# Sixteen-clip audio layer on one core: other steps let the table gathers go on GpSimd

## The reference

```python
q = (x @ Wq).reshape(b, n, HEADS, DIM) * DIM ** (-0.5)          # 8 heads of 64
sim = jnp.einsum('pbnhd,pkhd->pbnhk', qpk, pk_keys)             # two halves, 64 keys each
scores, idx = jax.lax.top_k(sim, 16)                            # 16 of 64 in each half
final_scores, pk_idx = jax.lax.top_k(all_sums, 16)              # 16 of the 256 pairs
final_scores = jax.nn.softmax(final_scores)
k = jnp.einsum('bnhk,bnhkd->bnhd', final_scores, keys_table[ind])
v = jnp.einsum('bnhk,bnhkd->bnhd', final_scores, values_table[ind])
out = causal_softmax(q, k) @ v, then @ Wo, plus the residual
```

## Time and profile before

| | |
|---|---|
| median of the three runs | 5366.33 us |
| the profiled execution's own time | 5371.56 us |
| its span | 5369.7 us |
| mean granted TensorE clock | 0.940 of full speed |
| the attention's first weighting, the last gather's start | 1104.4, 5266.4 us |
| busy share: TensorE, VectorE, ScalarE, GpSimd | 81%, 77%, 42%, 49% |
| gathers on GpSimd | 2528, mean 1016 ns |

### The profile page before, as it was taken

The page is one execution under the profiler, slowest core; times in us unless marked ns, Lnnn a source line. Parts: engine busy times, 40 slices in busy tenths (PEclk is TensorE's granted clock), DMA queues, the critical chain, the costliest instruction groups (busy, mean ns, idle before and its releaser), DMA issues.

```text
span 5369.7 us, 104279 instructions
## 1 busy us (share of the span) xinstructions
PE 4336.4 (81%) x28033; PEld 2830.8 (53%) x28033; DVE 4139.9 (77%) x16757; ACT 2279.4 (42%) x5575; POOL 2657.5 (49%) x2915
## 2 busy tenths in 40 slices
PE   5677775057889888888888888888888888888888
PEld 4555552024555555555555555555555555555556
DVE  4677776668888878887878888888888888878843
ACT  4333333023444444444444444444444444444444
POOL 0011111343566656566656656656656665656661
PEclk8999997578999999999999999999999999999998
DMA  1000002012323232323232323233332323232321
GB/s 45 1 0 0 0 0 54 24 48 61 100 78 104 78 100 77 102 79 101 77 99 78 101 77 105 86 92 89 94 91 86 97 84 99 81 101 77 104 77 53
DMA packets 160561, 389.31 MB, mean 73 GB/s; under 512 B 65847, under 2 KB 69943, under 8 KB 159612
## 3 DMA queue, kind: packets, MB, share of 16 engines
q1 hardware_dynamic: 78876, 215.14, 12.7%
q0 software_dynamic: 81120, 167.81, 12.0%
HBM read 379.87 MB, written 4.61 MB: 72 GB/s over the span
## 4 chain that ended last, share of the span: by engine, by line
DVE 28%; PE 23%; issue 17%; another core or an unknown queue 10%; ACT 4%; DVEq 1%; DMA 0%; ACTq 0%; POOL 0%; POOLq 0%
PE ps L1043 22%; DVE w L1763 6%; DVE topi L1585 4%; DVE miss L1705 2%; ACT ex L1391 2%; DVE top L1579 2%; DVE sc L1591 2%; DVE miss L1710 1%; DVE cs L1591 1%; DVE sm L1773 1%; DVE fin L1579 1%; PE ps L1238 1%; DVE left L1515 1%; DVE wmat L1559 1%
## 5 line engine op out<-in xcount | busy, mean ns | idle before, releaser
L1030 POOL DMA_INDIRECT rows<-table_dram,idxT x2528 | 2569.2, 1016 | 1783.8 <-issue 663.9
L1043 PE MATMUL ps<-w,dtab 128*128 128x375 f32 (+1 forms) x6144 | 1784.3, 424 | 15.4 <-issue 13.8
L1763 DVE SCALAR_TENSOR_TENSOR w<-ps,ex 128x750 f32<-128x750 f32 (+1 forms) x1152 | 1107.6, 961 | 526.5 <-remote 170.1
L1043 PEld LDWEIGHTS ps<-w,dtab 128*128 128x128 f32 x6144 | 1033.4, 198 | 401.7 <-issue 77.6
L1391 ACT ACTIVATE ex<-ps 128x750 f32<-128x750 f32 (+1 forms) x1152 | 947.6, 823 | 607.9 <-PE ps L1043 368.0
L1043 PE MATMUL ps<-rank_dense,half 128*128 128x375 bf16 (+1 forms) x2432 | 557.6, 320 | 223.8 <-DVE w L1763 177.8
L1043 PE MATMUL ps<-parts,half 128*128 128x375 bf16 x2176 | 547.7, 333 | 78.5 <-ACT ex L1391 50.2
L1043 PEld LDWEIGHTS ps<-rank_dense,half 128*128 128x128 bf16 x2432 | 209.0, 99 | 679.7 <-DVE w L1763 381.4
L491 POOL COPY states<-n_h 64x32 f32 (+1 forms) x375 | 76.8, 205 | 748.4 <-DVE n_h L480 748.4
L382 PE MATMUL ps<-which,bias 128*64 128x256 bf16 (+2 forms) x3123 | 397.5, 280 | 8.7 <-DVE which L461 8.7
L1585 DVE FIND_INDEX8 topi<-top,sc 125x8 uint32<-125x64 f32 x1536 | 306.5, 220 | 40.1 <-issue 38.7
(11 more groups left out here) (227 smaller groups left out, 6312.5 us busy)
## 6 DMA issues: line engine op xcount, KB each, us to landing
dtab<-dense_dram SPq DMA_DIRECT2D x256, 512.0 KB
dtab<-corner_dram SPq DMA_DIRECT2D x128, 512.0 KB
rows<-table_dram,idxT POOLq DMA_INDIRECT x2528
xin<-x_dram SPq DMA_DIRECT2D x16, 187.5 KB
early<-early_dram SPq DMA_DIRECT2D x1, 1800.5 KB, 9.0
half<-halves_dram POOLq DMA_DIRECT2D x1, 1680.0 KB, 12.8
rows_in<-hh SPq DMA_DIRECT2D x16, 93.8 KB, 2.2
rows_in<-uu SPq DMA_DIRECT2D x16, 93.8 KB, 2.2
```

Source lines behind the costliest of these rows:

```text
L1030: nc.gpsimd.indirect_dma_start(out=rows[:, PLACES[u] * GROUP + j, :], out_offset=None, in_=table[:, :], in_offset=bass.IndirectOffsetOnAxi ...
L1043: return nc.tensor.matmul(out_, lhsT, rhs, start=start, stop=stop, skip_group_check=open_bank)
L1763: nc.vector.scalar_tensor_tensor(w[:, p % 2, :, 0:wide], ps[:, 2:4, 0:wide], float(K), ex[:, p % 2, :, 0:wide], ALU.is_lt, ALU.mult).then_ ...
```

## The change

The even share of all events is replaced by a list. Every step's event 0 (weighting) and event 2 (exponents) lets one gather go, and the 14 gathers that are left over go with event 1 (rank sums) of steps 4, 9, 14, 19, 24, 28, 33, 38, 43, 48, 52, 57, 62 and 67. So 72 gathers go with the weighting, 72 with the exponents, 14 with the rank sums. Again 58 steps have two and 14 have three. Compared gather by gather, 56 keep their event, 88 go one event later, 12 two events later and 2 one event earlier.

```diff
 FIRST_PACED = 54
+THIRDS = [(i + 1) * STEPS // (GATHERS - 2 * STEPS + 1) for i in range(GATHERS - 2 * STEPS)]
+PACE = sorted([(p, e) for p in range(STEPS) for e in (0, 2)] + [(p, 1) for p in THIRDS])
 HEADS = NT * H
...
                     for j, t in enumerate(ts):
-                        at, event = divmod(i * (3 * STEPS) // GATHERS, 3)
+                        at, event = PACE[i]
                         if paced and event == 0:
                             pool.wait_ge(s_w, n * STEPS + (FIRST_PACED - STEPS + at))
```

## The result

| | before | after |
|---|---|---|
| median beside each other | 5371.47 us | 5388.56 us |
| smallest and largest of 14 runs | 5352.31, 5392.22 | 5373.19, 5407.72 |
| ratio, 95% interval | | 1.0031, 1.0017 to 1.0044 |
| span of the profiled execution | 5369.7 us | 5383.1 us |

A forecast was written before the change was run, and what follows sets the result against it. The prediction took the attention as bound by each step's loop over TensorE, ScalarE and VectorE, with no wait for gathers; all terms were 0 against 5371.6 us, carried to the median as 5366, range 5345 to 5386.

The forecast's parts named there:

- Instructions, releases, margins: GpSimd's program and TensorE's uses of units: same instruction counts, later gathers still land in time; both terms 0.
- Rival 3: At TensorE's uses of gathered units: releases come too late, 1 us in each of 15 batches, +15 us, 5381; chance 0.04.
- GpSimd's mean: Mean gather time on GpSimd: 1000 to 1090 ns expected (1016 before), with more gathers of 1.5 us and over.
- VectorE's slices: Slices behind the weighting on VectorE: gathers give way, slices do not; `miss` keeps 1211 to 1268 ns, time term 0.
- The step that failed: Timing of the 14 middle batches: dense engines' programs and durations do not depend on gathers, so term 0; ends -67 and +62.
- The prediction's last sign: Whole kernel: a change over 0.2% with unchanged clock and batch pattern would mean a missed link from gathers to dense steps.
- price of luck: Middle batches: ordinary scatter 10 us either way; a tilt of 1.3 us a batch gives 18 us.
- Rival 1: Middle batches dealt anew by changed timing: 5348 on the good side (chance 0.20), 5384 on the bad (0.13).
- Its own mark: Sign of Rival 1: middle batches' mean leaves 263.0 us by over 0.8 us while the clock of the stretch moves.

The follow-up runs named there:

- this list at 54: The changed kernel itself, with FIRST_PACED = 54 (paced gathers let go counted from 18 steps ahead): 5388.56 us, 1.0031 of the kernel before.

## Why the prediction was wrong

*Instructions, releases, margins: right.* The margins stayed: the seventh unit's smallest is 6.6 us, the eighth's 5.1, between the last gather's end and TensorE's first use. Rival 3 did not happen, and TensorE never waits for a gather in the kernel after. GpSimd's mean is 1017 ns, inside 1000 to 1090; gathers of 1.5 us and over did not become more, as the prediction had it, but fewer (140 against 150).

*VectorE's slices: right.* The row of `miss` keeps its mean in all kernels within 3 ns, with the longest runs of gathers too. In the kernel before, 163 of the 224 slices begin inside a gather and take 1221 ns in the mean and 1226 at the most; the other 61 take 1221 in the mean too. After, one slice of 224 takes 1289, over the 1268 of the earlier trace rows; the mean is the same:

```profile
L1707 DVE TENSOR_TENSOR miss<-codes,keycode 125x2048 uint16<-125x2048 uint16 x224 | 273.6, 1221 | 2.9
```

and without pacing:

```profile
L1705 DVE TENSOR_TENSOR miss<-codes,keycode 125x2048 uint16<-125x2048 uint16 x224 | 273.5, 1221 | 2.9
```

By the shared ports that the Trainium skill describes ("SBUF — State Buffer", section "SBUF: two separate sides") only VectorE could be held by a gather. The same section says that TensorE and ScalarE never wait on anyone there. The trace agrees for the durations and shows that it isn't the whole story of a gather: without pacing, ScalarE and TensorE stand still for 11 us beside a run.

*The step that failed* is the one that carried the sum: "nothing in the rows links a gather to the busy engines", and "what does not change cannot deal anew". I had looked at durations, and durations don't change. A gather's price appears only in starts, as idle time of all engines at once, which the page files under "another core or an unknown queue" (10% of the chain in the earlier trace rows, 11% after). With half of the gathers that entry is 1%, with plain DMAs it is gone from the chain, and without pacing it is 23%, in this order:

```profile
DVE 40%; PE 22%; issue 16%; ACT 2%; another core or an unknown queue 1%; DVEq 1%; DMA 0%; POOL 0%; ACTq 0%; POOLq 0%
```

```profile
DVE 42%; PE 23%; issue 14%; ACT 1%; DVEq 1%; DMA 0%; POOL 0%; ACTq 0%; POOLq 0%
```

```profile
another core or an unknown queue 23%; PE 23%; DVE 20%; issue 17%; ACT 3%; DVEq 0%; DMA 0%; ACTq 0%; POOL 0%; POOLq 0%
```

I had that row in hand and read past it. The term was put at 0. With half of the gathers a batch takes 235.3 us, so they cost this kernel 263.0 - 235.3 = 27.7 us a batch, 10% of the time. (With plain DMAs, on the faster chip, a batch takes 235.4 and the difference is the same; on the slower chip it is 34.3, as above.) An edit of their timing redistributes that sum. A tilt of it by 4% (17 of 27.7 x 15 = 416 us) is the whole result. The prediction's last sign named this case: a change over 0.2% with the same pattern of clock and batches would mean a missed link from the gathers to the dense steps.

*The wrong price of luck.* Rival 1 came near the outcome (5384 on its bad side) on the wrong ground, which is why it got 0.13. Its own mark did not come: the middle batches' mean moved by 0.6 us, not by over 0.8, and the clock of the stretch stayed at 0.97. It is no luck of the clock: most stalls keep to their steps and follow the gathers. The two traces differ by 13.4 us. In the middle batches the difference is 8.8, and the idle time in common grew there by (8.78 - 7.91) x 14 = 12 us, more than the whole of it; TensorE's busy time grew by 5.4 us.

*Why slower, and not faster?* The new list makes longer runs: in the middle batches 60% of the gathers stand in runs of five or more against 56%, 38% in runs of seven or more against 29%, and it gives 72 instead of 54 gathers to the weighting, the dearer of the two events that were run alone. Both point to slower. But the same list was faster than the old one a step earlier (5467 against 5498), and the old one lost 0.5% by one event's shift. So the runs show that gathers moved against the steps are worth up to 0.6%; that this list at 54 is on the bad side is measured and has two reasons that fit, neither of them isolated. No run used the rank sums alone.

## What to carry to other kernels

An engine that is on no chain can still slow the others: look at moments when all engines are idle together and ask what was in flight then, and test it once by leaving that work out. On this kernel that one experiment, half of the gathers, would have shown 9% where the page shows 0%. And with such a coupling, moving the work in time by an event or a step went either way here; a rest of a microsecond behind every third gather was a gain, behind every fourth it was none, and behind every one it cost 19%.

## What was not expected of the hardware

- Without pacing, behind 10 us of rest, the first seven indirect gathers of a run (1.25 us each) went unnoticed; then TensorE, VectorE and ScalarE stopped, for up to 11.5 us in the stretch shown, and went on when the run ended. That is no safe length: with at most four in a row and all 158 gathers a batch the kernel was as slow as before. `miss` slices under way were not stretched (1221 ns).
- Plain DMAs of the same size from GpSimd, in the same number and at the same places, don't do it: 4838 against 5375 us, with 0.54 against 0.94 us of GpSimd for each.
- A gap of 0.49 us filled by a memset gave no relief, gaps of 1.0 to 1.1 us behind every third gather gave 2.1%, behind every fourth nothing. What is used up in a run, and what gives it back, stays open.
- The granted clock falls with the stalls: 1.00 with 80 gathers a batch, 0.97 with 158, 0.93 with all of them on the weighting, 0.81 without pacing (middle batches).
